# Operand stacks of an attention kernel, laid out by halves of the tokens

## The reference

```python
q = _layernorm((x @ Wq.T).reshape(N, L, H, D).transpose(0, 2, 1, 3), gq, bq)
k = _layernorm((x @ Wk.T).reshape(N, L, H, D).transpose(0, 2, 1, 3), gk, bk)
scores = jnp.where(causal, jnp.einsum('nhld,nhmd->nhlm', q, k), NEG)
out = jnp.einsum('nhlm,nhmd->nhld', softmax(scores), v)
x = x + out @ Wo.T + bo
```

## Time and profile before

| | us |
|---|---|
| median of 3 runs | 3604.78 |
| lowest and highest | 3600.71, 3610.52 |
| the profiled execution | 3605.54 |
| its span, first to last instruction | 3603.8 |
| mean granted TensorE clock | 0.977 of full |

### The profile page before, as it was taken

The page is one execution under the profiler, slowest core; times in us unless marked ns, Lnnn a source line. Parts: engine busy times, 40 slices in busy tenths (PEclk is TensorE's granted clock), DMA queues, the critical chain, the costliest instruction groups (busy, mean ns, idle before and its releaser), DMA issues.

```text
span 3603.8 us, 78881 instructions
## 1 busy us (share of the span) xinstructions
PE 3270.5 (91%) x29880; PEld 2562.6 (71%) x29880; DVE 2740.6 (76%) x5880; ACT 2142.0 (59%) x6105; POOL 945.6 (26%) x656
## 2 busy tenths in 40 slices
PE   4998999989899898999989899899998989989898
PEld 3676776767777677776767767677676776867777
DVE  5887878777777777777777787787887878777775
ACT  3765656556565665646665466665665656566563
POOL 3340232312323222232212323023230232312220
PEclk7999999999999999999999999999999999999999
DMA  7003040120402104040040400404013040220400
GB/s 135 7 12 50 7 59 7 27 40 2 60 7 39 27 2 60 7 54 13 1 60 7 59 8 4 57 7 59 8 20 47 2 59 7 34 33 2 59 2 7
DMA packets 188985, 104.24 MB, mean 29 GB/s; under 512 B 16640, under 2 KB 188544, under 8 KB 188608
## 3 DMA queue, kind: packets, MB, share of 16 engines
q1 hardware_dynamic: 188608, 99.21, 18.1%
HBM read 65.62 MB, written 33.55 MB: 28 GB/s over the span
## 4 chain that ended last, share of the span: by engine, by line
PE 60%; ACT 12%; DMA 11%; DVE 10%; issue 4%; SPq 3%; POOL 1%; ACTq 0%; POOLq 0%; DVEq 0%
PE bank L721 15%; PE bank L732 9%; DMA stash<-part 8%; ACT prob L1018 7%; PE scores L708 6%; PE scores L789 4%; PE scores L709 4%; PE scores L838 4%; SPq L464 3%; PE scores L812 3%; DMA qkt<-stash 3%; PE scores L710 3%; PE bank L669 3%; PE scores L704 2%; PE bank L825 1%
## 5 line engine op out<-in xcount | busy, mean ns | idle before, releaser
L1018 ACT ACTIVATE prob<-scores,negmax 128x128 f32<-128x128 f32 (+3 forms) x2048 | 1059.6, 536 | 304.6 <-DVE negmax L1284 296.3
L1284 DVE TENSOR_REDUCE negmax<-scores 128x1 f32<-128x128 f32 (+3 forms) x2048 | 873.9, 483 | 121.8 <-PE scores L710 107.9
L721 PE MATMUL bank<-ident,prob 128*128 128x128 f32 x5120 | 739.2, 282 | 62.3 <-DVE probt L1292 40.5
L1292 DVE COPY probt<-bank 128x512 f32<-128x512 f32 x896 | 596.9, 684 | 189.4 <-PE bank L721 183.8
L721 PEld LDWEIGHTS bank<-ident,prob 128*128 128x128 f32 x5120 | 555.2, 143 | 179.2 <-issue 73.6
L710 PE MATMUL scores<-mask,ident 128*128 128x128 bf16 x2048 | 445.4, 230 | 0.0
L1018 ACT ACTIVATION_READ_ACCUMULATOR prob<-scores,negmax 128x1 f32 x2048 | 434.8, 212 | 0.0
L708 PE MATMUL scores<-khh,qt 128*128 128x256 f32 (+2 forms) x1024 | 416.2, 407 | 13.3 <-POOL kll L598 13.3
L539 POOL COPY rexp<-rsum 128x512 f32<-128x512 f32 x128 | 78.3, 612 | 1146.4 <-DVE rsum L1296 1146.4
L557 POOL TENSOR_TENSOR rq<-ssq,expo 128x32 f32<-128x32 f32 x64 | 352.3, 5523 | 72.6 <-DVE ssq L1256 47.5
L704 PE MATMUL scores<-qkt 96*128 96x128 bf16 (+3 forms) x1024 | 270.4, 323 | 98.0 <-DMA qkt<-stash 76.5
(11 more groups left out here) (185 smaller groups left out, 6023.7 us busy)
## 6 DMA issues: line engine op xcount, KB each, us to landing
qkt<-stash SPq DMA_DIRECT2D x384, 128.0 KB, 6.0
stash<-part SPq DMA_DIRECT2D x96, 256.0 KB, 5.7
x_in<-in_x_rows SPq DMA_DIRECT2D x16, 512.0 KB, 3.9
out_rows<-x SPq DMA_DIRECT2D x16, 512.0 KB, 6.5
r_d<-in_wd SPq DMA_DIRECT2D x1, 1024.0 KB, 7.4
r_gu<-in_wg SPq DMA_DIRECT2D x2, 512.0 KB, 4.5
r_gu<-in_wu SPq DMA_DIRECT2D x2, 512.0 KB, 5.6
r_wob<-in_wo SPq DMA_DIRECT2D x4, 128.0 KB, 5.2
```

The lines of the kernel that those rows point to most:

```text
L721: ins = nc.tensor.transpose(bank[4 + n % 2][:, q * P:(q + 1) * P], prob[:, u % 2, q, i * P:(i + 1) * P], ident[:, :])
L1018: nc.scalar.activation(prob[:, u % 2, q, 0:n], bank[q][:, 0:n], ACT.Exp, bias=negmax[:, a, u, q:q + 1], accum_out=sums[:, a, u, q:q + 1]). ...
L1284: nc.vector.tensor_reduce(negmax[:, a, u, M * part:M * part + M], scores[:, M * part:M * part + M, 0:n], axis=AX.X, op=ALU.max, negate=Tru ...
L1292: nc.vector.tensor_copy(probt[:, u % 2, i], bank[4 + n % 2][:, :]).then_inc(probt_dve.sem, 1)
```

## The change

`qkt` and `stash` get the halves of the tokens as an outer dimension: `qkt` is [96, 2, 32, 256], `stash` is [3 parts, 2 halves, 16 channels, 32 heads, 256 tokens]. In `stash` the 16 heads of a channel's half are then one run of 8 KB, and in a row of `qkt` too. A load of a slot has 16 runs of 8 KB where it had 256 of 512 bytes; number, bytes and target rows of the loads stay. A store is split by c into four DMAs of 64 KB, each of 8 heads x 16 channels x 512 bytes, because the order of the dimensions in `stash` is now channel, head, token. The counts of the stores' semaphores go up fourfold. A score with more than 256 columns reads two halves of `qkt`, so it is two matmuls into the same bank, one of 256 columns and one of the rest, with the same weights.

```diff
-    qkt = new("qkt", [SD, 2 * H, L], BF16)
+    qkt = new("qkt", [SD, 2, 2 * H, HALF], BF16)
...
-    stash = nc.dram_tensor("stash", (3, 4 * P, L), BF16, kind="Internal").ap()
+    stash = nc.dram_tensor("stash", (3, 2, D, 2 * H, HALF), BF16, kind="Internal").ap()
...
-    high_stored = Signal(sem("high_stored"), 2 * 16)
+    high_stored = Signal(sem("high_stored"), 2 * STORES * 16)
...
         def store_part(k, half, signal):
-            tokens = slice(half * 2 * P, (half + 1) * 2 * P)
-            sp.dma_start(stash[k].rearrange("(c p) l -> p c l", p=P)[:, :, tokens], part[:, k, :, tokens]).then_inc(signal.sem, 16)
+            tokens = slice(half * HALF, (half + 1) * HALF)
+            for c in range(4):
+                heads = slice(c * P // D, (c + 1) * P // D)
+                sp.dma_start(stash[k, half, :, heads].rearrange("d h l -> h d l"), part[:, k, c, tokens]).then_inc(signal.sem, 16)
 
         def load_slots(k, half):
-            tokens = slice(half * 2 * P, (half + 1) * 2 * P)
             for first, slots in ((0, QUERY_SLOTS[k]), (H, KEY_SLOTS[k])):
-                rows = stash[k][first * D:(first + H) * D].rearrange("(h d) l -> d h l", d=D)
                 for s in slots:
-                    sp.dma_start(qkt[s * D:(s + 1) * D, first:first + H, tokens], rows[:, :, tokens]).then_inc(stack_loaded[half].sem, 16)
+                    sp.dma_start(qkt[s * D:(s + 1) * D, half, first:first + H], stash[k, half, :, first:first + H]).then_inc(stack_loaded[half].sem, 16)
...
-            sp.wait_ge(high_stored.sem, high_stored.at(b, 16 * (half + 1)))
+            sp.wait_ge(high_stored.sem, high_stored.at(b, STORES * 16 * (half + 1)))
...
-                    mm(bank[q][:, 0:n], qkt[:, h, j * P:(j + 1) * P], qkt[:, H + h, 0:n], start=True, stop=False)
+                    tok = qkt[:, j // 2, h, j % 2 * P:(j % 2 + 1) * P]
+                    mm(bank[q][:, 0:min(n, HALF)], tok, qkt[:, 0, H + h, 0:min(n, HALF)], start=True, stop=False)
+                    if n > HALF:
+                        mm(bank[q][:, HALF:n], tok, qkt[:, 1, H + h, 0:n - HALF], start=False, stop=False)
```

More of the change, by code:

```diff
@@ L42 @@
 SPLITS = 6
+HALF = L // 2
+STORES = 4
 SD = SPLITS * D
@@ L282, in _build @@
     low_ready = Signal(sem("low_ready"), NT)
-    high_stored = Signal(sem("high_stored"), 2 * 16)
-    mid_stored = Signal(sem("mid_stored"), 2 * 16)
-    low_stored = Signal(sem("low_stored"), 2 * 16)
+    high_stored = Signal(sem("high_stored"), 2 * STORES * 16)
+    mid_stored = Signal(sem("mid_stored"), 2 * STORES * 16)
+    low_stored = Signal(sem("low_stored"), 2 * STORES * 16)
     stack_loaded = [Signal(sem(f"stack_loaded{half}"), 2 * SPLITS * 16) for half in range(2)]
@@ L476, in stack_rows @@
             store_part(2, half, low_stored)
-            sp.wait_ge(mid_stored.sem, mid_stored.at(b, 16 * (half + 1)))
+            sp.wait_ge(mid_stored.sem, mid_stored.at(b, STORES * 16 * (half + 1)))
             load_slots(1, half)
-            sp.wait_ge(low_stored.sem, low_stored.at(b, 16 * (half + 1)))
+            sp.wait_ge(low_stored.sem, low_stored.at(b, STORES * 16 * (half + 1)))
             load_slots(2, half)
@@ L755, in attend @@
                         pe.wait_ge(rest_ready.sem, rest_ready.at(b, NT))
-                        pe.wait_ge(high_stored.sem, high_stored.at(b, 32))
-                        pe.wait_ge(mid_stored.sem, mid_stored.at(b, 32))
-                        pe.wait_ge(low_stored.sem, low_stored.at(b, 32))
+                        pe.wait_ge(high_stored.sem, high_stored.at(b, 2 * STORES * 16))
+                        pe.wait_ge(mid_stored.sem, mid_stored.at(b, 2 * STORES * 16))
+                        pe.wait_ge(low_stored.sem, low_stored.at(b, 2 * STORES * 16))
                     else:
@@ L1000, in high_part_qk @@
             if b > 0 and t % 2 == 0:
-                act.wait_ge(high_stored.sem, high_stored.at(b - 1, 32))
+                act.wait_ge(high_stored.sem, high_stored.at(b - 1, 2 * STORES * 16))
             copy(part[:, 0, :, t * P:(t + 1) * P], bank[6 + t % 2].rearrange("p (c l) -> p c l", c=4)).then_inc(high_ready.sem, 1)
@@ L1014, in exps @@
             if a == 0 and u == 1 and part == 0:
-                act.wait_ge(mid_stored.sem, mid_stored.at(b, 32))
-                act.wait_ge(low_stored.sem, low_stored.at(b, 32))
+                act.wait_ge(mid_stored.sem, mid_stored.at(b, 2 * STORES * 16))
+                act.wait_ge(low_stored.sem, low_stored.at(b, 2 * STORES * 16))
             for q in range(M * part, M * part + M):
```

## The result

| | before | after |
|---|---|---|
| median, us | 3605.07 | 3611.94 |
| lowest and highest | 3600.08, 3610.52 | 3606.74, 3615.84 |
| runs | 20 | 20 |
| profiled execution, us | 3605.54 | 3606.77 |
| its span | 3603.8 | 3605.0 |

The ratio of after to before is 1.0019, with an interval of 1.0013 to 1.0026: 6.9 us slower, where 73 had been forecast. The interval leaves out 1, but the difference lies within the 0.3% that the prediction called no change.

What follows compares the result with a forecast made beforehand. The prediction took the DRAM round trip building the next batch's stacks as the bound. Per join +1.4 issue and 3 x 1.0 drain made +4.4, over 16 joins 70.4, plus scores 3, loads 0: 3678 us, range 3605 to 3725.

Steps and rivals of the forecast that it cites:

- What bounds the kernel: Round trip through DRAM building the next batch's operand stacks: 72.2 us idle before the 384-column score, 16 joins of 4.5 us.
- The loads: Loads from stash to qkt: rate follows the 16 rows reached, not run length; 1.07 us each, no change.
- Rival 3: Loads drain at 0.9 to 1.0 us, engines finishing long runs serving different rows; 3605 to 3645 us; chance 0.12.
- The stores: Four 64 KB stores per part's half instead of one DMA: issue and drain together add 4.4 us per join.
- Issue: SyncE's three extra store DMAs of part 1 stand ahead of the six loads: +1.4 us per join; others hidden.
- Drain: Four small stores take 1.9 us a part instead of 0.9: +1.0 for each of three parts waited for on the chain.
- The waits: Semaphore waits keep their places, only counts change; unit 0's transposes start 1.9 us later, at no cost.
- The score in two pieces: Score matmuls over 256 columns: 512 more matmuls with weight loads, 3 us taken, bounds nothing and 51 us.
- Rival 1: Long runs speed the loads to 0.43 us, 3517 us; faster than before from 0.2 us less per load; chance 0.13.
- Rival 2: The four stores drain together as fast as one, 292 GB/s; only +1.4 per join stays, 3630 us; chance 0.13.
- Rival 4: The 8 KB runs are still moved in short pieces; time unchanged, packet count would show it; no chance given.
- The signs named ahead: Loads 1.0 to 1.2 us apart at 105 to 125 GB/s, stores about 140, score idle near 140 us, low part 2 to 4 later.

Runs made afterwards that it cites:

- spread_rows: The kernel before with each load's 16 rows placed at every sixth of the 96 rows instead of adjacent: 3516.35 us.
- one_store_long: The kernel after with one store per part's half instead of four, loads still in 8 KB runs, output not the reference's: 3544.83 us.
- grouped kernels: The kernel before, and the one with one store and 8 KB loads, each with loads into like rows queued behind one another: 3629.60 and 3580.58 us.
- one_store_1k: The kernel after with one store per part's half and loads in 1 KB runs instead of 8 KB, output not the reference's: 3566.11 us.
- short_grouped: The kernel before, 512 B runs and one store, with loads into like rows queued behind one another: 3629.60 us.
- split_store_short: The kernel before with only the change's four stores per part's half, outermost count 8; loads in 512 B runs, scores in one piece: 3653.66 us.
- split_store_16: The kernel before with each store split in four by c in the old stash layout, outermost count 128: 3614.13 us.
- pieces_only: The kernel before with only qkt laid out by halves and scores over two halves in two matmuls: 3602.47 us.
- spread_rows_long: The kernel after with each load's 16 rows placed at every sixth of the 96 rows: 3556.66 us.

## Why the prediction was wrong

- **What bounds the kernel: right.** Take the round trip off the chain and the 72.2 us go, with 15 more around them (spread_rows, -85.2; its mean granted clock is 0.991 for 0.977).
- **The loads: the step that failed.** It took 1.07 us a load, unchanged, so nothing for them in the sum. By the landings a load of the change is some 0.09 us less (1.04 and 0.98 apart for 1.10 and 1.13), and 22 x 0.09 = 2.0 us a join. In the time of the kernel it is 42 us beside the four stores and 59.5 beside one (one_store_long). Rival 3 had the time, 3605 to 3645, and had been given 0.12; its reason, engines that run ahead into other rows, is Theory 2, to which the grouped kernels leave about a quarter of the gain (59.5 less 46). The error was one of evidence: "the rate follows the rows that the transfer reaches, not the run" rested on half a microsecond of `r_oa` at the start of the program, and on no pair that differs in the run alone. That row even spoke against it: `r_oa` came at 109 GB/s with a DMA share of 0.72, the loads at 117 with 1.24, so `r_oa` took some 38% less of the engines' time for a byte. one_store_1k makes a pair with before, but for the pieces of the scores and the order in `stash`, and it is 37 us faster. That rows count was right (spread_rows, short_grouped); that runs don't count was wrong. Rows and runs both count.
- **The stores: the second step, right in kind, too dear in drain.** Issue: 2.04 us on the chain, not 1.4, because an issue takes 0.57 with a gap of 0.04 and not the 0.47 of the earlier trace rows; four of them stand where one of 0.36 stood. Drain: +3.0 a join were taken, for three parts that drain alone. A part does take 1.53 us alone (262 kB at 171 GB/s) and not 0.9, but where it stands behind loads it added nothing (0.8 us in both kernels, by the landings). In this join -1.66 was measured from the first load to the last; with the loads' -2.0 that leaves some +0.3 for the three stores. In split_store_short, without the long loads, issue and drain cost 49.3 us; with 16 x 2.04 = 33 for the issue that leaves 16 for the drain, or 1.0 a join.
- **The sum, term by term.** 73 were forecast: 22 for the issues, 48 for the drain, 3 for the scores, nothing for the loads. The runs have 33, 16, nothing and -42.
- **Why half the rate.** The stores' DMA share of 0.58, and split_store_16 (same number, same size, +10 and not +49), are what the Trainium skill, DMA: Bandwidth & Descriptors, section Why a DMA increments its semaphore by 16 and not by 1, leads one to expect of an outermost count of 8: a DMA on 8 of 16 engines. The packets under 512 B agree, 8 a store and 16 where 128 is outermost. By it a part was to take 1.8 us; measured, 1.53.
- **The waits: they did change, without a price.** The transposes wait 18.0 us for stores in after; the idle time before them is 7.8 us more (70.1, and 62.3 for L721 in before's groups by shape), and that before the scores of all shapes 8.4 less (89.6 and 98.0). One gap lies ahead of the other and both end when the loads are in, as the prediction had it. That it costs nothing is read from these two sums; no run parts it.
- **The score in two pieces: 3 us forecast, nothing measured** (pieces_only).
- **Rival 1** fell as it was put: the loads didn't come to 0.43 us, nor to its break-even of 0.2 us less per load. But that was reckoned against 4.4 us for the stores, which came to some 3 (49.3 / 16), and with one store in place of four the kernel ends on that side (one_store_long, -59.5). **Rival 2** fell: 171 GB/s, not 292. **Rival 4** fell by the packets.
- **The signs named ahead.** Low part's landing 512.94 before, 516.86 after: +3.9, but this join's first store of part 1 is itself issued 2.6 later (486.78 and 489.40), so within the join +1.3, under the 2 to 4. First load after part 1's issue: +2.04 and not 1.4. Stores alone: 171 GB/s, nearer to the 140 than to the 290. Loads: 1.0 apart and 125 GB/s, at the edge of the bands named for the reading by rows; the bands were too wide for a load that counts 22 times in a join. The idle time at the scores: 64 and not 140, the sign that told.

## What to carry to other kernels

A change with two effects of opposite sign is priced at each sign by a pair of rows that differ in one thing alone: one short stretch that differs in size, place and neighbours is a bound, not a price. Before a layout is changed for longer runs, look which partitions a small transfer reaches: one slice with a step in place of a contiguous one (16 rows spread over 96) gave 2.4% here, and the change of layout as it was made gave nothing. And an outermost count of 8 in a DMA, the only one under 16 tried here, and three more DMAs on the queue that feeds the chain can take back what the longer runs bring.

## What the runs showed of the hardware

- **Where 16 rows lie** sets a load's rate: 117 GB/s for 16 adjacent rows, at least 193 for every sixth of 96, of the same 512 B runs. The Trainium skill, SBUF — State Buffer, section Door 1: The DMA port swizzle, has 16 adjacent rows on 4 of 16 ports; by its table every sixth of 96 rows reaches 13 or 14, with two rows at the most on one, so by its 27.2 GB/s a port an estimate of 8 x 27.2 = 218 GB/s. The trace doesn't test that: its 193 are what SyncE issued, at a DMA share of 0.65. For 16 adjacent rows it has 109 to 117 where the page has 104.
- **Neighbours in the queue**: loads into the same rows or rows that lie 32 apart, behind one another, cost 26 and 30 us (five such pairs in a half for one); with none there is a gain of 7 and 10. The same section has rows 32 apart on one port, and these runs agree.
- **Run length** counts above 512 B: 1.10, 1.03 and 0.98 us a load for 512 B, 1 KB and 2 KB into 16 rows, and windows of 117, 131 and 144 GB/s. The Trainium skill, DMA: Bandwidth & Descriptors, section Why small descriptors are slow (HBM only), names a fixed cost of about 3 cycles a packet; by it 2 KB over 512 B is an estimate of 1.13. By the landings it is 1.10 / 0.98 = 1.12 for the six loads and 1.13 / 0.96 = 1.18 for the four, which is near it; by the windows, with the store in them, 144 / 117 = 1.23.
- **Issuing** a DMA isn't one price: a train of four stores takes SyncE 1.90 us with 128 rows outermost and 2.42 with 8 heads outermost, and six loads 3.69 into every sixth row (spread_rows_long) and 2.77 into adjacent rows (after, from 491.85).
